# Four unread bf16 products per recurrent step, and one semaphore for both inputs of the cell scan

## The chip, the core and the metric

The kernel runs on one core of a Trainium2 chip. The time is device microseconds of that core, the median of three runs. The engines of a core are TensorE (PE for its products, PEld for its weight loads), VectorE (DVE), ScalarE (ACT), GpSimd (POOL) and SyncE (SP, which here only issues DMAs); each runs its own list of instructions and waits for others on semaphores.

## The reference

A graph of 6250 nodes with 256 features goes through four residual blocks: a weighted neighbour sum, a mixture of eight expert layers, a four-head graph attention, and an LSTM that walks over the 6250 nodes one after the other. Only the last one matters here:

```python
def step(carry, xp):                  # 6250 times, each on the h and c of the one before
    h, c = carry
    gates = xp + h @ W_hh.T           # 256 -> 1024
    i, f, g, o = jnp.split(gates, 4, axis=-1)
    c = sigmoid(f) * c + sigmoid(i) * tanh(g)
    h = sigmoid(o) * tanh(c)
    return ((h, c), h)
```

`xp` is `x @ W_ih.T` plus both biases for all nodes, computed ahead of the loop.

## The kernel before, in words

The kernel is a list of stages, one after the other: `stage_places`, `stage_scatter`, `stage_items` (sorting of edges), `stage_aggregate`, `stage_experts`, `stage_heads`, `stage_maxima`, `stage_attend`, `stage_project` (writes `xp` to HBM), `stage_lstm` (the recurrence) and `stage_finish`. The change is in `stage_lstm` alone.

`stage_lstm` gives each engine its own loop of 625 turns with 10 steps each (PER = CH * LU = 2 * 5). A step, engine by engine:

- TensorE first writes the `xp` row of the step into three PSUM banks (f, i and g, o; two sets of banks, used in turn) by three f32 products with a 128 x 128 selection matrix `sel` and 64 columns of `xp` (line 1160). Each is recorded as two weight loads and two matmuls, so six of each. Then it waits for `h_ready`, and adds h @ W_hh.T: the weights loaded into the array are h itself (one or two columns of it), the columns that stream are 64 columns of `ls_w`, and four such products lie side by side in the four 32-column parts of the array (`tile_position=(0, 32 * j)`). There are 8 of them for f (line 1167), 16 for i and g (1173) and 8 for o (1178), each recorded as two: 16, 32 and 16 matmuls. After each of the three blocks `gates_ready` goes up.
- VectorE transposes the f bank, the i/g bank and the o bank into SBUF (1229, 1233, 1235; each raises `turned`), waits for `f_mul` and for `ig_act`, runs one scan that makes the new cell state (1239), waits for `tc_ready` and writes the new h into the ring `ls_ht` (1242, raises `h_ready`).
- ScalarE takes tanh of f (1188, raises `f_act`), of i and g straight into the scan's input (1190, raises `ig_act`), of o (1192), of the new cell state (1194, raises `tc_ready`), and copies that state to the scan's input (1195). Every fifth step it copies five h to the history (1199).
- GpSimd multiplies tanh(f) by the old cell state into the scan's input (1147, raises `f_mul`).
- SyncE loads five rows of `xp` at a time into one half of a double buffer when `xp_used` says it is free.

Sigmoids are written as tanh of half the argument; the weights are scaled for that. PSUM banks 0 to 5 hold the gates; banks 6 and 7 are not used in this stage.

Of the kernel before, what the change touches and what calls it, by code (L numbers as in the profile page):

```python
# [14 lines left out]
BF16 = mybir.dt.bfloat16  # L15
I32 = mybir.dt.int32
ALU = mybir.AluOpType
ACT = mybir.ActivationFunctionType
# [3 lines left out]
P = 128  # L22
# [1082 lines left out]
def stage_lstm(nc, sb, sem, g):  # L1105
# [4 lines left out]
    tf_cols, ti_cols, to_cols = sb("ls_f_cols", [P, HD]), sb("ls_ig_cols", [P, HD]), sb("ls_o_cols", [P, HD])  # L1110
    tf, to, tc = sb("ls_tf", [P, 2]), sb("ls_to", [P, 2]), sb("ls_tc", [P, 2])
    SC = 5
    d = sb("ls_d", [P, 2, 2 * SC + 1])
    cell = sb("ls_cell", [P, 2 * SC])
    ht = sb("ls_ht", [P, 2 * LU, 2, 3])
    free = sb("ls_free", [P, 1])
    d1, d0 = d[:, 0, 1:2 * SC + 1], d[:, 1, 0:2 * SC]
    c_now = cell[:, SC - 1:2 * SC:SC]
    banks_f, banks_ig, banks_o = [[g["ps"][3 * s + k] for s in range(2)] for k in range(3)]
    w_loaded, zeroed, gates_ready, turned, f_act, f_mul, ig_act, scanned, tc_ready, h_ready, kept, xp_used = (sem("ls_" + n) for n in (  # L1120
        "w_loaded", "zeroed", "gates_ready", "turned", "f_act", "f_mul", "ig_act", "scanned", "tc_ready", "h_ready", "kept", "xp_used"))
    xp_in = [sem("ls_xp0"), sem("ls_xp1")]
    PER = CH * LU
    with nc.Block() as block:
# [15 lines left out]
        @block.gpsimd  # L1140
        def _(pool):
            pool.memset(free[:, :], 0.0).then_inc(kept, 2)
            pool.wait_ge(zeroed, 5)
            with pool.Fori(0, N // PER) as i:
                for k in range(PER):
                    pool.wait_ge(f_act, i * PER + (k + 1))
                    nc.gpsimd.tensor_tensor(d1[:, 2:2 * SC:SC], tf[:, :], c_now, ALU.mult).then_inc(f_mul, 1)  # L1147

        @block.tensor
        def _(pe):  # L1150
            pe.wait_ge(zeroed, 5)
            with pe.Fori(0, N // PER) as i:
                for k in range(PER):
                    q, u, s = k // LU, k % LU, k % 2
                    b = q % 2
                    if u == 0:
                        pe.wait_ge(xp_in[b], i * (CH // 2 * 16) + (q // 2 + 1) * 16)

                    for bank, lo in ((banks_f[s], HD), (banks_ig[s], 0), (banks_o[s], HD)):
                        x = nc.tensor.matmul(bank[:, 0:HD], sel[:, u, :], xp[:, b, lo:lo + HD], start=True, stop=False)  # L1160
                    if u == LU - 1:
                        x.then_inc(xp_used, 1)
                    pe.wait_ge(h_ready, i * PER + (k + 1))
                    v = (k - 1) % (2 * LU)
                    for c in range(2):
                        for j in range(4):
                            m = nc.tensor.matmul(banks_f[s][32 * j:32 * j + 1, 0:HD], ht[:, v, c, 1:2], w[:, c, j, HD:2 * HD],  # L1167
                                                 start=False, stop=c == 1, tile_position=(0, 32 * j))
                    m.then_inc(gates_ready, 1)
                    for r, lo in ((0, 0), (1, 2 * HD)):  # L1170
                        for c in range(2):
                            for j in range(4):
                                m = nc.tensor.matmul(banks_ig[s][32 * j:32 * j + 2, 0:HD], ht[:, v, c, 1 - r:3 - r], w[:, c, j, lo:lo + HD],  # L1173
                                                     start=False, stop=(r, c) == (1, 1), tile_position=(0, 32 * j))
                    m.then_inc(gates_ready, 1)
                    for c in range(2):
                        for j in range(4):
                            m = nc.tensor.matmul(banks_o[s][32 * j:32 * j + 2, 0:HD], ht[:, v, c, 0:2], w[:, c, j, 3 * HD:4 * HD],  # L1178
                                                 start=False, stop=c == 1, tile_position=(0, 32 * j))
                    m.then_inc(gates_ready, 1)  # L1180

        @block.scalar
        def _(act):
            act.wait_ge(zeroed, 5)
            with act.Fori(0, N // PER) as i:
                for k in range(PER):
                    act.wait_ge(turned, i * (3 * PER) + (3 * k + 1))
                    nc.scalar.activation(tf[:, :], tf_cols[:, 0:33:32], ACT.Tanh).then_inc(f_act, 1)  # L1188
                    act.wait_ge(turned, i * (3 * PER) + (3 * k + 2))
                    nc.scalar.activation(d[:, :, 2:3 + SC:SC], ti_cols[:, :].rearrange("p (c m) -> p m c", c=2)[:, 0:2, :], ACT.Tanh).then_inc(ig_act, 1)  # L1190
                    act.wait_ge(turned, i * (3 * PER) + (3 * k + 3))
                    nc.scalar.activation(to[:, :], to_cols[:, 1:34:32], ACT.Tanh)  # L1192
                    act.wait_ge(scanned, i * PER + (k + 2))
                    nc.scalar.activation(tc[:, :], c_now, ACT.Tanh).then_inc(tc_ready, 1)  # L1194
                    nc.scalar.copy(d1[:, 3:2 * SC:SC], c_now)
                    if k % LU == LU - 1:
                        v = k % (2 * LU) - (LU - 1)
                        act.wait_ge(h_ready, i * PER + (k + 2))
                        nc.scalar.copy(g["HIST"][:, :, ds(i * PER + (k - LU + 1), LU)], ht[:, v:v + LU, :, 1].rearrange("p u c -> p c u")).then_inc(kept, 1)

        @block.vector
        def _(dve):
            vec = nc.vector
            vec.memset(xp[:, :, :], 0.0).then_inc(zeroed, 1)
            vec.memset(sel[:, :, :], 0.0).then_inc(h_ready, 1)
            vec.memset(cell[:, :], 0.0)
            vec.memset(d[:, :, :], 0.0).then_inc(scanned, 1)
            dve.wait_ge(h_ready, 1)
            for j in range(4):
                for r in range(2):  # L1210
                    m = vec.tensor_copy(sel[:, :, 32 * j + r], g["ident"][:, 2 * j + r:2 * j + r + R * (LU - 1) + 1:R])
            m.then_inc(zeroed, 1)
            vec.memset(ht[:, :, :, :], 0.0)
            dve.wait_ge(scanned, 1)
            vec.memset(d1[:, 0:2 * SC:SC], 1.0)
            vec.memset(d0[:, 1:2 * SC:SC], 1.0)
            vec.memset(d0[:, 3:2 * SC:SC], 1.0)
            vec.memset(d0[:, 4:2 * SC:SC], 0.5)
            dve.wait_ge(w_loaded, 16)

            for lo, hi, scale in ((0, 2 * HD, 0.25), (2 * HD, 3 * HD, 0.5), (3 * HD, D, 0.25)):
                v = w[:, :, :, lo:hi].rearrange("p c j n -> p (c j) n")
                vec.tensor_scalar(v, v, scale, None, ALU.mult).then_inc(zeroed, 1)  # L1223
            dve.wait_ge(zeroed, 5)
            with dve.Fori(0, N // PER) as i:
                for k in range(PER):
                    s = k % 2
                    dve.wait_ge(gates_ready, i * (3 * PER) + (3 * k + 1))
                    vec.transpose(tf_cols[:, :], banks_f[s][:, 0:HD]).then_inc(turned, 1)  # L1229
                    if k % LU == 0:  # L1230
                        dve.wait_ge(kept, i * CH + (k // LU + 1))
                    dve.wait_ge(gates_ready, i * (3 * PER) + (3 * k + 2))
                    vec.transpose(ti_cols[:, :], banks_ig[s][:, 0:HD]).then_inc(turned, 1)  # L1233
                    dve.wait_ge(gates_ready, i * (3 * PER) + (3 * k + 3))
                    vec.transpose(to_cols[:, :], banks_o[s][:, 0:HD]).then_inc(turned, 1)  # L1235
                    dve.wait_ge(f_mul, i * PER + (k + 1))
                    dve.wait_ge(ig_act, i * PER + (k + 1))

                    vec.tensor_tensor_scan(cell[:, :], d0, d1, 0.0, ALU.mult, ALU.add).then_inc(scanned, 1)
                    dve.wait_ge(tc_ready, i * PER + (k + 1))  # L1240

                    vec.scalar_tensor_tensor(out=ht[:, k % (2 * LU), :, 1], in0=to[:, :], scalar=1.0, in1=tc[:, :],  # L1242
                                             op0=ALU.add, op1=ALU.mult).then_inc(h_ready, 1)
# [135 lines left out]
def build(nc, ins, out):  # L1379
    with ExitStack() as ctx:  # L1380
# [24 lines left out]
        with ExitStack() as items:  # L1405
# [21 lines left out]
            stage(stage_project)  # L1427
        g["HIST"] = keep("history", [P, 2, N])
        stage(stage_lstm)
        stage(stage_finish)  # L1430

# [12 lines left out]
```

## Time and profile before

| | |
|---|---|
| median of 3 runs | 31179.84 us (31170.26 to 31184.28) |
| profiled execution | 31181.4 us, span 31179.7 us |
| PE / PEld busy over the span | 84% / 70% |
| DVE / ACT / POOL busy | 36% / 27% / 25% |
| mean granted TensorE clock | 0.631 of full speed |
| recurrent stage, first to last instruction | about 10466 to 31014 us, 6250 steps |

The page divides the span into 40 slices of 780 us; a digit is the busy share of a slice in tenths, and PEclk is the granted clock of TensorE in tenths. The clock has two levels, 1.2 and 2.4 GHz, shown as 0.50 and 1.00; a value between is a mixture over the stretch. PE's busy time counts a matmul from its start to the end of its latency, so PE can show 100% while the array itself has pauses.

### The profile page before, as it was taken

The page shows a single profiled execution, that of the slowest core. Times are in us where ns is not written, and L with a number is a line of the kernel's source. Part 1 is how long each engine was busy: PE and PEld are TensorE (multiplying, and loading weights), DVE is VectorE, ACT ScalarE, POOL GpSimd, SP SyncE. Part 2 cuts the span into 40 slices and gives each one's busy share as a digit, 9 for nine tenths or more (in the row PEclk, how much of TensorE's full clock was granted, in tenths as well). Part 3 has the DMA queues.
Part 4 walks back from the last instruction along what each step waited for, and adds up shares of the span by engine and source line. Part 5 has one row for each costly group of instructions (what it writes and reads, how often), then busy time and mean ns, then how long its engine had stood idle before and what let it go on. Part 6 is the DMA issues. An engine that isn't in the chain of part 4 may idle for free. (4 is left out here: it accounts for less than half of the span.)

```text
span 31179.7 us, 1124934 instructions
## 1 busy us (share of the span) xinstructions
PE 26082.7 (84%) x456492; PEld 21913.3 (70%) x456597; DVE 11210.6 (36%) x40897; ACT 8537.5 (27%) x40793; POOL 7747.7 (25%) x12838
## 2 busy tenths in 40 slices
PE   0002556788777799999999999999999999999998
PEld 0002334333665688888888888888888888888887
DVE  7002333777555333333333333333333333333334
ACT  0000001688111132222222222232222222222322
POOL 1776771677776000000000000000000000000000
PEclk9998778999888655555555555555555555555555
DMA  0002331000333000000000000000000000000000
GB/s 36 1 1 71 104 105 24 7 2 2 97 99 93 33 1 1 1 1 1 1 1 1 1 1 1 1 1 1 1 1 1 1 1 1 1 1 1 1 1 9
DMA packets 370440, 557.74 MB, mean 18 GB/s; under 512 B 177610, under 2 KB 254830, under 8 KB 369006
## 3 DMA queue, kind: packets, MB, share of 16 engines
q0 software_dynamic: 263728, 458.62, 5.9%
q1 hardware_dynamic: 106686, 98.81, 1.0%
q8 instruction: 11, 0.18, 0.0%
q14 instruction: 15, 0.12, 0.0%
HBM read 496.64 MB, written 60.32 MB: 18 GB/s over the span
## 5 line engine op out<-in xcount | busy, mean ns | idle before, releaser
L1160 PE MATMUL banks<-ls_xp,ls_sel 128*128 128x64 f32 x37500 | 9641.6, 430 | 18.2 <-DVE ls_w L1223 18.2
L1160 PEld LDWEIGHTS banks<-ls_xp,ls_sel 128*128 128x128 f32 x37500 | 8466.7, 325 | 1376.1 <-issue 1376.1
L1173 PE MATMUL banks<-ls_w,ls_ht 128*2 128x64 f32 x200000 | 6735.4, 311 | 0.0
L1147 POOL TENSOR_TENSOR ls_d<-ls_tf,ls_cell 128x2 f32<-128x2 f32 x6250 | 1241.9, 199 | 19305.7 <-ACT ls_tf L1188 19305.7
L1173 PEld LDWEIGHTS banks<-ls_w,ls_ht 128*2 128x2 f32 x200000 | 5585.4, 127 | 0.0
L1229 DVE STREAM_TRANSPOSE ls_f_cols<-banks 128x64 f32<-128x64 f32 x6250 | 1561.5, 250 | 7590.1 <-PE banks L1167 7590.1
L1178 PE MATMUL banks<-ls_w,ls_ht 128*2 128x64 f32 x100000 | 4068.7, 311 | 0.0
L436 PE MATMUL banks<-ag_rows,ag_pick 128*128 128x256 f32 x3328 | 1204.8, 526 | 3392.9 <-DMA ag_rows<-y_table,ag_idx 3359.0
L1167 PE MATMUL banks<-ls_w,ls_ht 128*1 128x64 f32 x100000 | 3777.1, 299 | 0.0
L1188 ACT ACTIVATE ls_tf<-ls_f_cols 128x2 f32<-128x2 f32 x6250 | 1286.8, 206 | 8783.7 <-DVE ls_f_cols L1229 8776.7
L436 PEld LDWEIGHTS banks<-ag_rows,ag_pick 128*128 128x128 f32 x3328 | 831.5, 262 | 3765.6 <-DMA ag_rows<-y_table,ag_idx 2759.9
L1178 PEld LDWEIGHTS banks<-ls_w,ls_ht 128*2 128x2 f32 x100000 | 2918.7, 127 | 0.0
L1233 DVE STREAM_TRANSPOSE ls_ig_cols<-banks 128x64 f32<-128x64 f32 x6250 | 1561.5, 250 | 3771.8 <-PE banks L1173 3771.8
L1167 PEld LDWEIGHTS banks<-ls_w,ls_ht 128*1 128x1 f32 x100000 | 1975.0, 103 | 736.4
L1190 ACT ACTIVATE ls_d<-ls_ig_cols 128x4 f32<-128x4 f32 x6250 | 1313.6, 210 | 3849.5 <-DVE ls_ig_cols L1233 3849.5
L1235 DVE STREAM_TRANSPOSE ls_o_cols<-banks 128x64 f32<-128x64 f32 x6250 | 1561.5, 250 | 1105.2 <-PE banks L1178 1105.2
L389 POOL DMA_INDIRECT at_rows<-wh_table,at_idx x1664 | 1743.2, 1048 | 511.1 <-issue 477.3
L389 POOL DMA_INDIRECT mx_rows<-alpha_dst_table,mx_idx x1664 | 1657.0, 996 | 507.7 <-issue 459.8
L329 POOL DMA_INDIRECT rec_table<-st_rec,st_idx x1560 | 1495.1, 958 | 1034.4 <-ACT st_idx L304 559.4
L389 POOL DMA_INDIRECT ag_rows<-y_table,ag_idx x1664 | 1582.0, 951 | 515.8 <-issue 497.9
L1192 ACT ACTIVATE ls_to<-ls_o_cols 128x2 f32<-128x2 f32 x6250 | 1278.3, 205 | 1353.1 <-DVE ls_o_cols L1235 1353.1
L1242 DVE SCALAR_TENSOR_TENSOR ls_ht<-ls_to,ls_tc 128x2 f32<-128x2 f32 x6250 | 1017.3, 163 | 1695.1 <-ACT ls_tc L1194 1695.1
(256 smaller groups left out, 19365.3 us busy)
## 6 DMA issues: line engine op xcount, KB each, us to landing
ag_rows<-y_table,ag_idx POOLq DMA_INDIRECT x1664, 2.7
mx_rows<-alpha_dst_table,mx_idx POOLq DMA_INDIRECT x1664, 2.3
at_rows<-wh_table,at_idx POOLq DMA_INDIRECT x1664, 2.8
projections<-xp_out SPq DMA_DIRECT2D x7, 3584.0 KB, 10.4
rec_table<-st_rec,st_idx POOLq DMA_INDIRECT x1563, 2.1
ls_xp<-projections SPq DMA_DIRECT2D x1250, 20.0 KB
rec_table<-zero POOLq DMA_DIRECT2D x5, 2496.0 KB, 20.9
rec_part<-rec_table SPq DMA_DIRECT2D x5, 2496.0 KB, 19.9
```

What stands on the lines that cost most here:

```text
L329: pool.indirect_dma_start(g["rec"][k], bass.IndirectOffsetOnAxis(ap=idx[:, h, u % SH:u % SH + 1], axis=0), recs[:, h, u % SH, :], None).th ...
L389: pool.indirect_dma_start(rows[:, u, :], None, table, bass.IndirectOffsetOnAxis(ap=idx[:, u // HU, u % HU:u % HU + 1], axis=0)).then_inc(g ...
L436: m = nc.tensor.matmul(sums[k], pick[:, u, :], rows[:, u, :], start=u == 2 * k, stop=u == 2 * k + 1)
L1160: x = nc.tensor.matmul(bank[:, 0:HD], sel[:, u, :], xp[:, b, lo:lo + HD], start=True, stop=False)
L1167: m = nc.tensor.matmul(banks_f[s][32 * j:32 * j + 1, 0:HD], ht[:, v, c, 1:2], w[:, c, j, HD:2 * HD], start=False, stop=c == 1, tile_positi ...
L1173: m = nc.tensor.matmul(banks_ig[s][32 * j:32 * j + 2, 0:HD], ht[:, v, c, 1 - r:3 - r], w[:, c, j, lo:lo + HD], start=False, stop=(r, c) == ...
L1178: m = nc.tensor.matmul(banks_o[s][32 * j:32 * j + 2, 0:HD], ht[:, v, c, 0:2], w[:, c, j, 3 * HD:4 * HD], start=False, stop=c == 1, tile_po ...
L1188: nc.scalar.activation(tf[:, :], tf_cols[:, 0:33:32], ACT.Tanh).then_inc(f_act, 1)
L1190: nc.scalar.activation(d[:, :, 2:3 + SC:SC], ti_cols[:, :].rearrange("p (c m) -> p m c", c=2)[:, 0:2, :], ACT.Tanh).then_inc(ig_act, 1)
L1229: vec.transpose(tf_cols[:, :], banks_f[s][:, 0:HD]).then_inc(turned, 1)
L1233: vec.transpose(ti_cols[:, :], banks_ig[s][:, 0:HD]).then_inc(turned, 1)
L1235: vec.transpose(to_cols[:, :], banks_o[s][:, 0:HD]).then_inc(turned, 1)
```

## The change

- A bf16 tile `wake` of 128 x 512 is added and set to 1.0 once, ahead of the loop.
- In each step, after the three `xp` products and ahead of the wait for `h_ready`, TensorE issues four bf16 products: one column of `wake` as the weights, 512 columns of `wake` streaming, each in another 32-column part of the array, into four rows of PSUM bank 6. Nobody reads bank 6 and no semaphore is raised.
- `f_mul` (POOL) and `ig_act` (ACT) become one semaphore `scan_in`, raised once by each in each step; the scan waits once, for `2 * (k + 1)` instead of twice for `k + 1`.

```diff
+    wake = sb("ls_wake", [P, 512], BF16)
...
-                    nc.gpsimd.tensor_tensor(d1[:, 2:2 * SC:SC], tf[:, :], c_now, ALU.mult).then_inc(f_mul, 1)
+                    nc.gpsimd.tensor_tensor(d1[:, 2:2 * SC:SC], tf[:, :], c_now, ALU.mult).then_inc(scan_in, 1)
...
                     if u == LU - 1:
                         x.then_inc(xp_used, 1)
+                    for j in range(4):
+                        nc.tensor.matmul(g["ps"][6][32 * j:32 * j + 1, :], wake[:, 0:1], wake[:, :], start=True, stop=True, tile_position=(0, 32 * j))
                     pe.wait_ge(h_ready, i * PER + (k + 1))
...
-                    nc.scalar.activation(d[:, :, 2:3 + SC:SC], ti_cols[:, :].rearrange("p (c m) -> p m c", c=2)[:, 0:2, :], ACT.Tanh).then_inc(ig_act, 1)
+                    nc.scalar.activation(d[:, :, 2:3 + SC:SC], ti_cols[:, :].rearrange("p (c m) -> p m c", c=2)[:, 0:2, :], ACT.Tanh).then_inc(scan_in, 1)
...
             vec.memset(ht[:, :, :, :], 0.0)
+            vec.memset(wake[:, :], 1.0)
...
-                    dve.wait_ge(f_mul, i * PER + (k + 1))
-                    dve.wait_ge(ig_act, i * PER + (k + 1))
+                    dve.wait_ge(scan_in, i * (2 * PER) + (2 * k + 2))
```

## Rows read from the trace of the kernel before

**Rows 1.** The page's 40 slices: TensorE granted clock, in tenths.
```profile
PEclk9998778999888655555555555555555555555555
```
**Rows 2.** Stretch, its length, busy PE, PEld, DVE, ACT, POOL; then clock, DMA share, GB/s.
```profile
10105.00:10130.00 25.00, 21.70 (x51) 9.31 (x49) 9.04 (x14) 0.00 (x0) 0.00 (x0) 1.00 0.06 24
...
10466.00:31014.00 20548.00, 20541.70 (x437500) 18447.89 (x437500) 6367.92 (x31268) 6146.59 (x33121) 1241.86 (x6250) 0.50 0.00 1
```
**Rows 3.** Timeline of one step: start, duration, engine, line, operation, count, idle before.
```profile
20000.22 1.54 PE L1160 MATMUL banks<-ls_xp,ls_sel 128*128 128x64 f32 x6
...
20000.53 0.17 DVE L1239 TENSOR_TENSOR_SCAN ls_cell<-ls_d 128x10 f32<-128x10 f32 x1
...
20000.75 0.19 ACT L1194 ACTIVATE ls_tc<-ls_cell 128x2 f32<-128x2 f32 x1
...
20000.98 0.16 DVE L1242 SCALAR_TENSOR_TENSOR ls_ht<-ls_to,ls_tc 128x2 f32<-128x2 f32 x1 [0.27 <-ACT ls_tc L1194]
...
20001.69 0.60 PE L1167 MATMUL banks<-ls_w,ls_ht 128*1 128x64 f32 x16
...
20002.07 1.08 PE L1173 MATMUL banks<-ls_w,ls_ht 128*2 128x64 f32 x32
20002.36 0.25 DVE L1229 STREAM_TRANSPOSE ls_f_cols<-banks 128x64 f32<-128x64 f32 x1 [1.23 <-PE banks L1167]
20002.65 0.20 ACT L1188 ACTIVATE ls_tf<-ls_f_cols 128x2 f32<-128x2 f32 x1 [1.62 <-DVE ls_f_cols L1229]
...
20002.92 0.65 PE L1178 MATMUL banks<-ls_w,ls_ht 128*2 128x64 f32 x16
20002.93 0.20 POOL L1147 TENSOR_TENSOR ls_d<-ls_tf,ls_cell 128x2 f32<-128x2 f32 x1 [3.09 <-ACT ls_tf L1188]
20003.22 0.25 DVE L1233 STREAM_TRANSPOSE ls_ig_cols<-banks 128x64 f32<-128x64 f32 x1 [0.60 <-PE banks L1173]
20003.50 0.21 ACT L1190 ACTIVATE ls_d<-ls_ig_cols 128x4 f32<-128x4 f32 x1 [0.65 <-DVE ls_ig_cols L1233]
...
20003.51 1.54 PE L1160 MATMUL banks<-ls_xp,ls_sel 128*128 128x64 f32 x6
...
20003.81 0.18 DVE L1239 TENSOR_TENSOR_SCAN ls_cell<-ls_d 128x10 f32<-128x10 f32 x1
```
**Rows 4.** The same timeline where a loop turn of ten steps begins.
```profile
20004.26 0.16 DVE L1242 SCALAR_TENSOR_TENSOR ls_ht<-ls_to,ls_tc 128x2 f32<-128x2 f32 x1 [0.27 <-ACT ls_tc L1194]
20004.54 0.21 ACT L1199 COPY history<-ls_ht 128x10 f32 x1 [0.22 <-DVE ls_ht L1242]
20004.96 1.28 ACT L1188 ACT_TABLE_LOAD   x1 [0.21 <-issue]
...
20006.25 0.20 ACT L1188 ACTIVATE ls_tf<-ls_f_cols 128x2 f32<-128x2 f32 x1
```
**Rows 5.** Timeline, four thin products of one group alone.
```profile
20011.93 0.33 PE L1173 MATMUL banks<-ls_w,ls_ht 128*2 128x64 f32 x4
```
**Rows 6.** Timeline, fourteen 128-column products at clock 1.00, then at clock 0.50.
```profile
5045.92 1.69 PE L124 MATMUL banks<-ident,moe_v 128*128 128x128 f32 x14
...
10150.92 3.25 PE L124 MATMUL banks<-ident,xp_xn 128*128 128x128 f32 x14 [24.21 <-DVE xp_xn L102]
```
**Rows 7.** Timeline at clock 1.00, two bf16 products of 512 columns, then one.
```profile
6101.59 0.59 PE L797 MATMUL banks<-mx_ident,mx_pen 128*128 128x512 bf16 x2
...
6104.51 0.38 PE L797 MATMUL banks<-mx_ident,mx_pen 128*128 128x512 bf16 x1 [0.60 <-ACT mx_pen L785]
```
**Rows 8.** By line and form, the fourteen of Rows 6: count, busy us, mean ns of one.
```profile
L124 PE MATMUL banks<-ident,moe_v 128*128 128x128 f32 x14 | 1.7, 272 | 0.0
...
L124 PE MATMUL banks<-ident,xp_xn 128*128 128x128 f32 x14 | 3.2, 425 | 24.2 <-DVE xp_xn L102 24.2
```
**Rows 9.** By line and form, 16000 to 20000 us: one thin product, and ScalarE's table loads.
```profile
L1173 PE MATMUL banks<-ls_w,ls_ht 128*2 128x64 f32 x38944 | 1311.5, 311 | 0.0
...
L1188 ACT ACT_TABLE_LOAD x121 | 155.2, 1283 | 25.6 <-issue 25.6
```

More of the change, by code:

```diff
@@ L1119, in stage_lstm @@
     banks_f, banks_ig, banks_o = [[g["ps"][3 * s + k] for s in range(2)] for k in range(3)]
-    w_loaded, zeroed, gates_ready, turned, f_act, f_mul, ig_act, scanned, tc_ready, h_ready, kept, xp_used = (sem("ls_" + n) for n in (
-        "w_loaded", "zeroed", "gates_ready", "turned", "f_act", "f_mul", "ig_act", "scanned", "tc_ready", "h_ready", "kept", "xp_used"))
+    w_loaded, zeroed, gates_ready, turned, f_act, scan_in, scanned, tc_ready, h_ready, kept, xp_used = (sem("ls_" + n) for n in (
+        "w_loaded", "zeroed", "gates_ready", "turned", "f_act", "scan_in", "scanned", "tc_ready", "h_ready", "kept", "xp_used"))
     xp_in = [sem("ls_xp0"), sem("ls_xp1")]
```

## The prediction

> **What bounds the kernel now.** I read the page's slices first [rows 1]. PEclk changes between 7 and 9 up to the thirteenth slice, falls to 5 at the fifteenth and stays there. The stretches say it exactly [rows 2]: the recurrent stage takes 20548 us, two thirds of the span, PE has a record open in practically all of it, and the granted clock is 0.50, the level of 1.2 GHz. 20548 us over 6250 steps is 3.287 us a step (the steps counted here by POOL's 6250 products). Elsewhere the same engine gets 1.00 (2.4 GHz) with less recorded work: 87% PE busy in 10105 to 10130 us; and the slices at 7 and 8 are mixtures of both levels.
>
> Then the timeline of one step [rows 3]. The xp products of a step start at 0.22 (us behind 20000), the recurrent products at 1.69, the next xp products at 3.51: 1.47 us for one block and 1.82 for the other, with nothing between. The new h starts at 0.98 and ends at 1.14, yet the products that need it start at 1.69. So h waits for TensorE 0.5 us in every step: the loop is bound by TensorE's own work at the low level, not by the chain through the other engines.
>
> Inside the two blocks: the six xp products start (1.54 - 0.42) / 5 = 0.22 apart (0.42 for one, from a like product in [rows 8]), though 64 columns need less; their 128-column weight loads pace them. Fourteen products with the same loads take 3.25 us at the low level and 1.69 at the high one [rows 6]; with one duration of 0.42 and 0.27 [rows 8] taken off, they are 0.217 and 0.109 apart, so this pace follows the clock. The 32 i/g products fill 2.07 to 2.92: 8 groups of four, 0.106 a group; a group alone [rows 5] lasts 0.33 against 0.311 for one product [rows 9], so the four start within 0.02 and run side by side. The 16 groups are 1.70 us of the 1.82.
>
> **The four products of ones.** They stand behind the xp products and ahead of the wait for h, so at the low level, where h is already there, they are on TensorE's path in full. Two bf16 products of 512 columns at the high level take 0.59 us together, one alone 0.38 [rows 7]: 0.21 apart. Each of the new ones streams as many columns; twice that, 0.43, at the low level, no row of before has it. Do the four overlap? They use the four column parts as [rows 5] do, so I take one duration and 0.02: 0.23 high, 0.43 to 0.45 low. In series it would be 0.85 and 1.71; these are the ends. Their weight load is one column, like line 1167's, and costs nothing that shows there. Bank 6 is nobody's, and the added VectorE fill of `wake` happens once, ahead of 6250 steps: nothing.
>
> So all depends on whether the extra columns lift the clock. In a step of before the array has columns to process for 16 x 0.106 + 6 x 0.106 = 2.33 of 3.29 us; half of the xp block is pauses between weight loads, which PE's busy row hides behind latencies. The stretch at 1.00 is one of wide products one after the other (51 in 25 us, half a microsecond each, 87% busy) [rows 2]. The change puts an unbroken run of 0.43 us right ahead of the recurrent groups, in 2.76 of 3.71 us. I take the clock to rise and to stay up, since at the high level the step is shorter and the same columns come more often.
>
> The Trainium skill ("TensorE: Matmul & The Clock Gate", section "What's actually happening") says "the default state is throttled, and activity releases the throttle". Taken for recorded busy time, that speaks against this change: [rows 2] has PE recorded busy for 20548 us at 0.50, so what counts is not what PE's row shows, and one-column weights might count for little as well. By it the sum would be the rival "clock stays low" below. Whoever counts streaming columns gets the forecast.
>
> **The step at the high level, along the chain.** Time 0 is the first f product. Low: 12 groups to the first o product take 2.92 - 1.69 = 1.23, that is 12 x 0.106 less 0.04. High: the i/g block's last group starts at 11 x 0.053 - 0.03 = 0.55. A thin product lasts 0.31 at the low level; a 128-column one went from 0.42 to 0.27 [rows 8], about half of the streaming and little of the latency, so 0.24: the i/g block ends at 0.80. The transpose of i/g follows 0.07 later (2.07 + 7 x 0.106 + 0.31 = 3.12; it starts at 3.22, so 0.07 to 0.10): 0.87. From there all is VectorE and ScalarE and does not follow TensorE's clock [rows 3]: transpose to scan 3.81 - 3.22 = 0.59, scan to tanh(c) 0.22, to the new h 0.23, its 0.16, and 0.07 from its end to the first product (as PE to DVE; before it was hidden, 0.03 to 0.10). Sum 0.87 + 0.59 + 0.22 + 0.23 + 0.16 + 0.07 = 2.14 us. The f side is earlier: f ends at 0.40, transpose 0.47, POOL's product 0.57 later (2.93 - 2.36) at 1.04, done 1.24, against 1.41 for ig_act. The o side too: its last product ends at 1.02, and by the f side's delay (2.65 - 2.36) plus 0.07 its tanh starts at 1.38, while tanh(c) is due at 1.68.
>
> **One semaphore in place of two.** tanh of i/g ends at 3.71 and the scan starts at 3.81, 0.10 later; after tanh(c), a single wait, h starts 0.98 - 0.94 = 0.04 later. The merge removes one standing wait of VectorE: between 0 and 0.07. I take 0.04. At the low level it is worth nothing (h has 0.5 us of slack); at the high level it counts: 2.10. Behind the waiting scan stands only h's own product, behind that the next transpose, so nothing new is held; POOL and ACT raise it once each per step and neither can be a step ahead, since both wait for transposes behind the scan.
>
> **Once in ten steps** ScalarE loads its tables [rows 4, 9]: 121 in 4000 us, 1.28 us each. The load starts 0.70 behind h's start and tanh(f) 1.99 behind it. At the low level h's 0.5 us of slack and the longer products hide it. At the high level tanh(f) would be due at 0.23 + 0.47 + 0.29 = 0.99 behind h's start; the product on POOL then ends at 1.99 + 0.28 + 0.20 = 2.47 and the scan starts at 2.5 rather than at 0.23 + 1.42 = 1.65: 0.85 us late, 0.085 a step. The history copy ends at 0.49, before 0.99: free. So 2.10 + 0.085 = 2.19.
>
> **What is late next is close.** TensorE's own work at the high level: groups 0.85 and 0.12 around them, xp 6 x 0.109 and 0.15 (0.19 at the low level, 1.47 - 6 x 0.213), wake 0.23: 2.00 us. It stays just under the chain's 2.10; the quartet fits in the time in which PE would wait for h. I take 2.20 for both. Saved: 3.287 - 2.20 = 1.087 us, 6250 times: 6794 us. 31181.4 - 6794 = 24387; the profiled execution is 1.6 us over the median of three, so the two are the same here. **Forecast: 24390 us.** Its own range is 2.05 (chain with the full 0.07, TensorE 2.00) to 2.42 a step, 23450 to 25800.
>
> **Rivals.**
> - *The clock stays low.* The quartet is then pure load on the engine that bounds: 3.287 + 0.43 = 3.71 us a step, +2690 us, 33870. It decides as soon as the level is 0.50, from the first step. For it: 20548 us at 0.50 under full recorded load, and weights of one column. Against: four parts of the array used side by side with all 128 rows, and 512 columns without a pause. In series it would be +10690, 41870; [rows 5] speak against that. Chance 0.17.
> - *The thin products don't get faster with the clock,* because issuing them binds: a group stays at 0.106. TensorE's step is 2.00 + 16 x 0.053 = 2.85, above the chain (2.10 + 11 x 0.053 = 2.68): 31181 - 6250 x 0.437 = 28450. For it: each group issues eight instructions. Against: the four of a group start within 0.02. Chance 0.14. The Trainium skill ("TensorE: Matmul & The Clock Gate", "Back-to-back issue gap") gives small matmuls a floor of about 25 ns from start to start, 64 x 0.025 = 1.6 us for a step's thin products, an estimate near this rival's 1.7; [rows 5] contradict it within a group, no row of before tests it over many at the high level.
> - *The quartet runs in series at the high level:* TensorE 2.00 + 0.64 = 2.64: 27140. Chance 0.05.
> - *The clock changes to and fro* as in the slices at 7 and 8 [rows 1]: half at each, (24390 + 33870) / 2 = 29130. Chance 0.06.
> - *Nothing changes* (a low clock, with the quartet in time that is free): 0.01.
>
> **How the numbers follow.** Forecast 0.57. Faster by over 0.2%, about what a measurement here can tell: 0.57 + 0.14 + 0.05 + 0.06 = 0.82; slower 0.17; same 0.01. The range from 23300 to 29500 holds all of the faster cases but the edges; left out is the slower one.
>
> **What would show it.** PEclk 1.00 through the recurrent stage; thin groups 0.053 apart; the four products of ones within 0.25 us; a gap on PE between them and the f products, ended by h; the scan 0.06 behind tanh of i/g; one step in ten longer by 0.85 us. PEclk at 0.50 with xp to f 1.90 apart would prove me wrong as a whole; groups at 0.106 with PEclk 1.00 in the size.

## The result and the profile after

The changed kernel takes 24358.47 us (median of 4, 24356.56 to 24366.54) against 31180.4 for the kernel before: a ratio of 0.7813, 95% interval 0.7799 to 0.7827. Forecast were 24390. Ahead of and behind the recurrence nothing moved: the first h is written at 10474 us as against 10476 us before, and the difference of 6825 us between the spans (31179.7 and 24354.7) lies in the recurrent stage.

First the stretch of that stage, with the columns of [rows 2], and the page's clock by slices:

```profile
10466.00:24190.00 13724.00, 13239.33 (x462500) 10810.16 (x462500) 6649.67 (x31251) 6599.39 (x33121) 1233.77 (x6250) 1.00 0.01 2
```
```profile
PEclk9999877789999888799999999999999999999999
```

13724 us over 6250 steps is 2.196 us a step, at a granted clock of 1.00 where it was 0.50 [rows 2]. Now the timeline of TensorE at the start of the stage, where the clock changes:

```profile
10469.43 1.54 PE L1161 MATMUL banks<-ls_xp,ls_sel 128*128 128x64 f32 x6 [18.19 <-DVE ls_w L1227]
10470.90 0.60 PE L1165 MATMUL banks<-ls_wake 128*1 128x512 bf16 x4
10471.28 0.65 PE L1170 MATMUL banks<-ls_w,ls_ht 128*1 128x64 f32 x16
10471.71 1.07 PE L1176 MATMUL banks<-ls_w,ls_ht 128*2 128x64 f32 x32
10472.56 0.65 PE L1181 MATMUL banks<-ls_w,ls_ht 128*2 128x64 f32 x16
10473.14 1.11 PE L1161 MATMUL banks<-ls_xp,ls_sel 128*128 128x64 f32 x6
10474.18 0.39 PE L1165 MATMUL banks<-ls_wake 128*1 128x512 bf16 x4
10474.39 0.40 PE L1170 MATMUL banks<-ls_w,ls_ht 128*1 128x64 f32 x16
...
10475.39 0.88 PE L1161 MATMUL banks<-ls_xp,ls_sel 128*128 128x64 f32 x6
10476.20 0.39 PE L1165 MATMUL banks<-ls_wake 128*1 128x512 bf16 x4
```

The first step is as slow as every step of before: six xp products in 1.54 us, sixteen thin ones in 0.65 (0.60 in [rows 3]). The second step's xp products take 1.11, the third's 0.88: the clock rises after one step with a quartet in it and has no further change until the stage is over. The quartet is recorded as 0.60 us at the low level and 0.39 at the high one.

The timeline of one plain step in the middle, on all engines, answers to [rows 3]:

```profile
20003.22 0.39 PE L1165 MATMUL banks<-ls_wake 128*1 128x512 bf16 x4
20003.30 0.16 DVE L1245 SCALAR_TENSOR_TENSOR ls_ht<-ls_to,ls_tc 128x2 f32<-128x2 f32 x1 [0.27 <-ACT ls_tc L1197]
...
20003.52 0.40 PE L1170 MATMUL banks<-ls_w,ls_ht 128*1 128x64 f32 x16
...
20003.74 0.63 PE L1176 MATMUL banks<-ls_w,ls_ht 128*2 128x64 f32 x32
...
20004.18 0.41 PE L1181 MATMUL banks<-ls_w,ls_ht 128*2 128x64 f32 x16
...
20004.44 0.25 DVE L1237 STREAM_TRANSPOSE ls_ig_cols<-banks 128x64 f32<-128x64 f32 x1 [0.20 <-PE banks L1176]
...
20004.52 0.88 PE L1161 MATMUL banks<-ls_xp,ls_sel 128*128 128x64 f32 x6
...
20004.96 0.18 DVE L1242 TENSOR_TENSOR_SCAN ls_cell<-ls_d 128x10 f32<-128x10 f32 x1
20005.17 0.21 ACT L1197 ACTIVATE ls_tc<-ls_cell 128x2 f32<-128x2 f32 x1
...
20005.41 0.16 DVE L1245 SCALAR_TENSOR_TENSOR ls_ht<-ls_to,ls_tc 128x2 f32<-128x2 f32 x1 [0.27 <-ACT ls_tc L1197]
20005.63 0.22 PEld L1170 LDWEIGHTS banks<-ls_w,ls_ht 128*1 128x1 f32 x16 [0.21 <-DVE ls_ht L1245]
```

From h to h it is 20005.41 - 20003.30 = 2.11 us. Note who waits now: the weight load at 20005.63 has an idle time before it that h ended, while before h was ready half a microsecond ahead of TensorE. The bound has moved from TensorE's work to the chain through all engines.

And the step with the table load, by three starts of h on VectorE:

```profile
19996.13 0.16 DVE L1245 SCALAR_TENSOR_TENSOR ls_ht<-ls_to,ls_tc 128x2 f32<-128x2 f32 x1 [0.27 <-ACT ls_tc L1197]
19998.24 0.16 DVE L1245 SCALAR_TENSOR_TENSOR ls_ht<-ls_to,ls_tc 128x2 f32<-128x2 f32 x1 [0.27 <-ACT ls_tc L1197]
20001.19 0.16 DVE L1245 SCALAR_TENSOR_TENSOR ls_ht<-ls_to,ls_tc 128x2 f32<-128x2 f32 x1 [0.27 <-ACT ls_tc L1197]
```

2.11, then 2.95: 0.84 us more, once in ten steps.

### The profile page after: what moved, and what is told of

The parts are those of the page before. It is cut to its first block and busy times, and to the rows that moved or that the text cites. A ratio compares the mean times of both kernels' runs of the same rounds, so it can differ in the third digit from the quotient of the medians.

```text
span 24354.7 us, 1174935 instructions
## 1 busy us (share of the span) xinstructions
PE 18767.2 (77%) x481492; PEld 14260.6 (59%) x481597; DVE 11493.8 (47%) x40898; ACT 8989.8 (37%) x40793; POOL 7736.8 (32%) x12838
## 5 line engine op out<-in xcount | busy, mean ns | idle before, releaser
L1161 PE MATMUL banks<-ls_xp,ls_sel 128*128 128x64 f32 x37500 | 5508.6, 283 | 84.3 <-DVE ls_w L1227 18.2
L1161 PEld LDWEIGHTS banks<-ls_xp,ls_sel 128*128 128x128 f32 x37500 | 4654.0, 191 | 854.6 <-issue 198.6
L1176 PE MATMUL banks<-ls_w,ls_ht 128*2 128x64 f32 x200000 | 3930.9, 219 | 0.0
L1176 PEld LDWEIGHTS banks<-ls_w,ls_ht 128*2 128x2 f32 x200000 | 3093.2, 85 | 0.0
L1170 PE MATMUL banks<-ls_w,ls_ht 128*1 128x64 f32 x100000 | 2520.5, 218 | 414.2 <-DVE ls_ht L1245 414.1
L1181 PE MATMUL banks<-ls_w,ls_ht 128*2 128x64 f32 x100000 | 2534.7, 219 | 0.6 <-issue 0.6
L1165 PE MATMUL banks<-ls_wake 128*1 128x512 bf16 x25000 | 2419.3, 377 | 0.0
L1170 PEld LDWEIGHTS banks<-ls_w,ls_ht 128*1 128x1 f32 x100000 | 1404.0, 82 | 1653.6 <-DVE ls_ht L1245 1630.7
L1181 PEld LDWEIGHTS banks<-ls_w,ls_ht 128*2 128x2 f32 x100000 | 1697.2, 85 | 0.8 <-issue 0.8
L802 PE MATMUL banks<-mx_diag,mx_pick 128*128 128x512 f32 x3328 | 1566.5, 593 | 0.0
```

The source lines that it names most:

```text
L802: m = nc.tensor.matmul(ps[u % 8][:, :], pick[:, u, :], diag[:, u, :, :].rearrange("p h e -> p (h e)"), start=False, stop=True)
L1165: nc.tensor.matmul(g["ps"][6][32 * j:32 * j + 1, :], wake[:, 0:1], wake[:, :], start=True, stop=True, tile_position=(0, 32 * j))
```

## The experiments

Twelve kernels ran, in three groups of four, the first and third on chip 0, the second on chip 14. The kernel before, run beside them, takes 32054, 31175 and 32142 us. The difference lies ahead of the recurrence; one of the stages that gather rows by indirect DMA shows it (3000 to 4000 us: 104 GB/s in the trace of before, 91 in the first group). The recurrence at the low level took 20548 us in the trace of before and 20539 us in that of the first kernel below, where the kernel as a whole is 3% slower, so I compare the length of the recurrence and its steps.

**The merged semaphore alone.**

```diff
-                    for j in range(4):
-                        nc.tensor.matmul(g["ps"][6][32 * j:32 * j + 1, :], wake[:, 0:1], wake[:, :], start=True, stop=True, tile_position=(0, 32 * j))
```

> The merged semaphore without the four products. My theory (all of the gain is TensorE's clock, and at the low level TensorE bounds the step): the clock stays at 0.50, a step stays at 3.287 us, 31180 us within 0.2%. Rival (the wait of the scan was worth part of it): a shorter step at 0.50, up to 0.07 us of 3.287, so down to 30740.

32063.75 us beside 32054 for the kernel before, all four executions within 18 us. The recurrent stage:

```profile
11362.00:31901.00 20539.00, 20537.85 (x437429) 18444.37 (x437428) 6120.22 (x31246) 6069.19 (x33122) 1232.96 (x6249) 0.50 0.00 1
```

Clock 0.50 and 3.287 us a step: at the low level the merge is worth nothing, so the gain comes from the products of ones.

**The four products, with the two semaphores of before.**

```diff
+                    dve.wait_ge(f_mul, i * PER + (k + 1))
+                    dve.wait_ge(ig_act, i * PER + (k + 1))
-                    dve.wait_ge(scan_in, i * (2 * PER) + (2 * k + 2))
```

> The four products with the two semaphores of before. Theory: the clock is 1.00 through the recurrence, and the merge is worth 0.04 us of the chain in nine steps of ten, so 24358 + 6250 x 0.04 = 24600. Bounds: 24360 (the merge is worth nothing) and 24800 (0.07 in every step). Rival (TensorE's own 2.03 us bounds the step, not the chain): no difference to the changed kernel.

25632.46 us on that chip, a recurrence of 14102 us at clock 1.00. Against 13724 that is 378 us, 0.06 a step: a plain step takes 2.18 us instead of 2.11, the one with the table load 2.95 as before. Two rows of VectorE show where:

```profile
20003.84 0.25 DVE L1237 STREAM_TRANSPOSE ls_ig_cols<-banks 128x64 f32<-128x64 f32 x1 [0.20 <-PE banks L1176]
...
20004.44 0.18 DVE L1243 TENSOR_TENSOR_SCAN ls_cell<-ls_d 128x10 f32<-128x10 f32 x1
```

Transpose to scan is 0.60 (0.59 in [rows 3]); merged it is 20004.96 - 20004.44 = 0.52. So the merge is worth 0.07 in a plain step (0.04 was forecast, 0.07 its upper bound) and nothing in the long one, where the scan waits for POOL's product. The rival, that TensorE bounds the step, is out: the merge would then show nothing.

**One product instead of four.**

```diff
-                    for j in range(4):
+                    for j in range(1):
```

> One of the four products of ones, in one column part of the array, with the merged semaphore; it streams as long as the four did side by side. Theory A (what lifts the clock is that columns stream, however wide the array is used): clock 1.00, 24360. Theory B (the part of the array in use decides, so a quarter is too little): clock 0.50 and 0.43 us more a step, 31180 + 2670 = 33850.

25245.52 us where the kernel before takes 32054. The recurrence:

```profile
11350.00:25074.00 13724.00, 13228.92 (x443678) 10707.84 (x443677) 6649.69 (x31245) 6595.75 (x33120) 1233.20 (x6249) 1.00 0.01 2
```

13724 us at clock 1.00, to the microsecond that of the changed kernel. One column part of the array is enough; the width in use did not decide. Three of the four products are ballast. They cost nothing, since they run beside the first.

**The products only ahead of the loop.**

```diff
+            for j in range(128):
+                nc.tensor.matmul(g["ps"][6][32 * (j % 4):32 * (j % 4) + 1, :], wake[:, 0:1], wake[:, :], start=True, stop=True, tile_position=(0, 32 * (j % 4)))
             with pe.Fori(0, N // PER) as i:
...
-                    for j in range(4):
-                        nc.tensor.matmul(g["ps"][6][32 * j:32 * j + 1, :], wake[:, 0:1], wake[:, :], start=True, stop=True, tile_position=(0, 32 * j))
```

> The products of ones stand 128 times ahead of the loop (32 groups, 14 us at the low level) and not at all in a step; merged semaphore. Theory A (at the high level a step takes 2.11 us and not 3.29, so its own products come often enough to hold the level; only the start needs help): clock 1.00 to the end, 24360 + 10. Theory B (each step needs the products, the thin ones count for little): the clock falls to 0.50 soon after the loop begins, 31190.

25253.9 us, four executions within 23 us. The burst, the first steps and the whole stage:

```profile
11343.40 9.19 PE L1154 MATMUL banks<-ls_wake 128*1 128x512 bf16 x128 [18.07 <-DVE ls_w L1227]
11352.51 0.88 PE L1163 MATMUL banks<-ls_xp,ls_sel 128*128 128x64 f32 x6
```
```profile
11355.00:25079.00 13724.00, 11825.36 (x437426) 10198.70 (x437425) 6649.67 (x31246) 6595.88 (x33120) 1233.26 (x6249) 1.00 0.01 2
```

The same 13724 us, with not one product of ones in 6250 steps. In this loop, which has no gap of microseconds, the level holds itself: the kernel's own work, one step in 2.11 us, keeps it; only to rise from the low level did it need help.

That has a consequence for the kernel before, and its runs beside the experiments show it. Of 27, 25 are at mean clocks of 0.62 to 0.63; one of the first group took 25736.94 us at 0.929, and one 30256.16 us at 0.698. No trace of these two is kept, but 25737 us is close to the 25632 of the same two semaphores with the quartet. By that the kernel before can run its recurrence at the high level; it seldom gets there.

**Columns in the quartet: 256 and 128 instead of 512.**

```diff
-                        nc.tensor.matmul(g["ps"][6][32 * j:32 * j + 1, :], wake[:, 0:1], wake[:, :], start=True, stop=True, tile_position=(0, 32 * j))
+                        nc.tensor.matmul(g["ps"][6][32 * j:32 * j + 1, 0:256], wake[:, 0:1], wake[:, 0:256], start=True, stop=True, tile_position=(0, 32 * j))
```

> The four products stream 256 columns instead of 512. If the clock is lifted all the same, the time is that of the changed kernel (the chain bounds, a shorter quartet frees nothing): 25250 on a chip with the slower other stages. If it is too little, the clock stays at 0.50 and a step takes 3.287 + 0.22 = 3.51 us: 1400 us over the kernel before, 33450. In between, executions that differ from one another.

24360.11 us, four executions within 6 us. The clock rises 14 us, or four steps, later than in the changed kernel, and then stays:

```profile
10474.00:10488.00 14.00, 14.00 (x297) 12.43 (x298) 4.03 (x21) 3.33 (x21) 0.79 (x4) 0.50 0.02 4
10488.00:24196.00 13708.00, 13035.38 (x462130) 10754.98 (x462130) 6643.09 (x31226) 6594.50 (x33099) 1232.73 (x6245) 1.00 0.01 2
```

> The four products stream 128 columns instead of 512. With 256 the clock rose about six steps later than with 512. If the columns in a step decide when the clock rises: it rises later still, or in some executions only; once it has risen it stays, 2.11 us a step. Then either 24360 to 24500, or values up to 31500 that differ from run to run. If any extra work is enough: 24360 as with 256 columns.

With 128 columns three executions took 32763 to 32784 us at clock 0.62 and one 25357 at 0.926. The profiled one stayed low from end to end:

```profile
11454.00:32617.00 21163.00, 21162.75 (x462425) 19060.94 (x462424) 6134.32 (x31244) 6101.09 (x33118) 1243.31 (x6249) 0.50 0.00 1
```

21163 / 6250 = 3.386 us a step, 0.10 over the 3.287 of before. Here my slow rival happened: the price of a quartet that does not lift the clock. A quarter of the 0.43 us that I put on the full quartet is 0.107. The full quartet itself stood at the low level in one step only, the changed kernel's first: 10471.28 - 10470.90 = 0.38 us, so 0.43 was somewhat high.

**Two quartets.**

```diff
-                    for j in range(4):
-                        nc.tensor.matmul(g["ps"][6][32 * j:32 * j + 1, :], wake[:, 0:1], wake[:, :], start=True, stop=True, tile_position=(0, 32 * j))
+                    for j in range(8):
+                        nc.tensor.matmul(g["ps"][6][32 * (j % 4):32 * (j % 4) + 1, :], wake[:, 0:1], wake[:, :], start=True, stop=True, tile_position=(0, 32 * (j % 4)))
```

> Eight products of ones a step instead of four, else the changed kernel. It measures how near TensorE's own work is to the bound. When h did not make it wait (third step of the changed kernel) TensorE's step was 0.21 + 1.00 + 0.81 = 2.02 us against the chain's 2.11. Theory: a second quartet adds 0.21, so a plain step takes 2.24 us, the step with the table load stays at 2.95, and the recurrence takes 6250 x 0.9 x 0.13 = 730 us more than with one quartet. Rival (the wait for h hides the quartets whatever their number): no difference.

26260.76 us, beside 31175 for the kernel before on that chip. A plain step takes 2.24 us, as expected, and the long one 2.95. But the recurrence takes 15595 us, where 13724 + 730 = 14450 were forecast. At 125 of the 625 turns of the loop TensorE stands still for some 5 us. Without these gaps ten steps take 22.97 us; each gap costs (15595 - 625 x 22.97) / 125 = 9.9 us with the slow steps behind it. TensorE's timeline and the DMA queues (12000 to 24000 us) show why:

```profile
10630.40 0.40 PE L1181 MATMUL banks<-ls_w,ls_ht 128*2 128x64 f32 x16
10635.75 1.54 PE L1161 MATMUL banks<-ls_xp,ls_sel 128*128 128x64 f32 x6 [4.96 <-issue]
10637.22 1.02 PE L1165 MATMUL banks<-ls_wake 128*1 128x512 bf16 x8
10638.92 0.60 PE L1170 MATMUL banks<-ls_w,ls_ht 128*1 128x64 f32 x16 [0.68 <-issue]
```
```profile
q8 instruction: 880, 14.42, 0.6%
```

Nothing that the profile shows makes TensorE wait for these 5 us; the queue by which instructions are loaded, which has no entry in this stretch of the changed kernel, moves 14 MB. Behind the gap the clock is low (1.54 for six xp products) and rises again.

**As many instructions, but short ones.**

```diff
+                    for j in range(4):
+                        nc.tensor.matmul(g["ps"][6][32 * j:32 * j + 1, 0:16], wake[:, 0:1], wake[:, 0:16], start=True, stop=True, tile_position=(0, 32 * j))
```

> The quartet of the changed kernel and four more products of only 16 columns. The two-quartet kernel had 14 MB of instruction DMA on TensorE's queue in 12 ms and gaps of 5 us, the changed kernel none. Theory (the stalls come from the number of instructions in TensorE's ten-step body, not from the time they take): as many instructions as with two quartets, so the same fetches and gaps in about 250 of 625 turns, with plain steps of 2.11 to 2.15 us: 24358 + 250 x 7 = 26100, less up to some hundred. Rival (the stalls come with the longer quartet): no fetches, 24400.

25836 us twice and 28428 and 28451 us, on a chip where the kernel before takes 32142. Plain steps of 2.11 us, and fetches again:

```profile
q8 instruction: 355, 5.82, 0.2%
```

So the number of instructions in the body brings the gaps, not the time they take. The profiled execution, one of the shorter two, has 49 gaps of some 5 us; they cost (14216 - 13724) / 49 = 10.0 us each. The 250 turns of the forecast were too many, since with two quartets it was 125. Why the executions differ, and why this one has fewer gaps than with two quartets, is open.

**Fifty steps in the body of every engine's loop.**

```diff
-CH = 2
+CH = 10
```

> The loop body holds 50 steps instead of 10 (CH = 10), else the changed kernel. Theory: the tables are loaded once per turn of the loop, 125 times instead of 625, and each load costs the step 2.95 - 2.11 = 0.84 us: 420 us less than the changed kernel on the same chip (25250 becomes 24830 where its other stages are as slow as in the last group of runs). Rival (the long step comes from the turn of the loop or from the history copy, or fetching a body five times as long costs time): the same time or more.

25746.65 us where the kernel before takes 31175: not 420 us less than the changed kernel but 1388 more. My theory of the load was right in its size and wrong in what a longer body costs. Queues from 12000 to 24000 us, and the gap at a turn of the loop:

```profile
q8 instruction: 3062, 50.17, 1.8%
...
q14 instruction: 1186, 9.72, 0.3%
```
```profile
20011.60 1.54 PE L1161 MATMUL banks<-ls_xp,ls_sel 128*128 128x64 f32 x6 [4.63 <-issue]
```

The step at a turn takes 9.4 us, the next two 3.7 and 2.6, and steps in between lose up to a microsecond.

**Fifty steps, and the products only ahead of the loop.**

```diff
-CH = 2
+CH = 10
...
-                    for j in range(4):
-                        nc.tensor.matmul(g["ps"][6][32 * j:32 * j + 1, :], wake[:, 0:1], wake[:, :], start=True, stop=True, tile_position=(0, 32 * j))
+            for j in range(128):
+                nc.tensor.matmul(g["ps"][6][32 * (j % 4):32 * (j % 4) + 1, :], wake[:, 0:1], wake[:, :], start=True, stop=True, tile_position=(0, 32 * (j % 4)))
```

> No product of ones in a step, 128 of them ahead of the loop, and the body of 50 steps. If both effects are as thought, they don't disturb each other: clock 1.00 throughout, a plain step 2.11 us, 125 table loads: as the 50-step body with quartets, 24830 on a chip with the slower other stages. If the clock falls somewhere, each step behind it takes 3.287 us.

30881.69 us. This is the run that tells what the quartet in each step is for:

```profile
10582.61 0.41 PE L1181 MATMUL banks<-ls_w,ls_ht 128*2 128x64 f32 x16
10587.52 1.54 PE L1163 MATMUL banks<-ls_xp,ls_sel 128*128 128x64 f32 x6 [4.51 <-issue]
...
10595.15 1.54 PE L1163 MATMUL banks<-ls_xp,ls_sel 128*128 128x64 f32 x6
```
```profile
10480.00:30714.00 20234.00, 19494.31 (x437424) 17425.20 (x437424) 6154.43 (x31246) 5516.31 (x32619) 1236.32 (x6249) 0.54 0.02 5
```

The clock falls behind the first gap at a turn, and without quartets it comes back only now and then: mean clock 0.54. The trace has 15 later stretches at the high level, each 106 us long: one turn of fifty steps, from just behind one gap to the next. Why the clock rises behind some gaps and not behind others is open. With quartets and the same gaps it was 0.94 (the fifty-step kernel above), back after each within some steps.

**A longer body for ScalarE alone: 30 and 40 steps.**

```diff
-            with act.Fori(0, N // PER) as i:
-                for k in range(PER):
+            AP = 30
...
+            with act.Fori(0, N // AP) as i:
+                steps(i * AP, AP)
+            steps(N // AP * AP, N % AP)
```

> ScalarE's loop alone gets a body of 30 steps (208 turns and ten steps behind them); TensorE's body keeps its ten. Theory (a table load at each turn of ScalarE's loop costs 0.84 us, and what made the 50-step body slow was fetching TensorE's instructions): 209 loads instead of 625, 416 x 0.84 = 350 us less: 24358 becomes 24010 on a chip where the changed kernel takes 24358, no instruction DMA in the recurrence. Rival (a longer body of any engine has to be fetched anew at each turn): stalls of some us at each of 208 turns, slower than the changed kernel.

25012.07 us where the kernel before takes 32141.63, a ratio of 0.7782 (0.7771 to 0.7793). The recurrence takes 13411 us at clock 1.00, 313 less than the changed kernel's 13724, and the instruction queues have no entry from 12000 to 24000 us:

```profile
11434.00:24845.00 13411.00, 13204.71 (x462425) 10805.51 (x462425) 6649.94 (x31245) 6158.17 (x32704) 1233.72 (x6249) 1.00 0.01 2
```

Forecast were 350 less. Table loads now come once in 30 steps; but two of those 30, where the other engines' loops of ten turn and the history is copied, take 2.20 instead of 2.11, which the load had covered: 417 x 0.09 = 37 us.

> The same with 40 steps in ScalarE's body (156 turns and ten steps). If 40 steps still need no fetching: 157 loads, 468 x 0.84 = 390 us less, 23970. If they do: instruction DMA in the recurrence and one stall of 3 us or more at each turn, which eats what is saved, about 24400.

25692.56 us, a recurrence of 14078: slower than the changed kernel's. One step in forty takes 5.1 us:

```profile
20018.93 0.21 ACT L1204 COPY history<-ls_ht 128x10 f32 x1 [0.22 <-DVE ls_ht L1251]
20021.55 1.28 ACT L1193 ACT_TABLE_LOAD   x1 [2.41 <-issue]
```
```profile
20024.02 0.40 PE L1170 MATMUL banks<-ls_w,ls_ht 128*1 128x64 f32 x16 [2.91 <-DVE ls_ht L1251]
```
```profile
q14 instruction: 666, 5.46, 0.2%
```

The load stands 2.41 us behind the copy instead of 0.21 [rows 4]: ScalarE's own body has to be fetched. Between 30 and 40 steps lies its end. The fetch costs the clock too: TensorE idles for 2.8 to 3.2 us at each of 155 turns, and each time the granted clock falls to 0.50 for some steps (0.97 over the stage). With 30 steps no idle time between TensorE's products reaches 0.8 us in the recurrence, and the clock stays at 1.00.

The Trainium skill ("Runtime: NRT & Kernel Launch", "Instruction fetch mechanics") gives the instruction memory as 32 KiB for most engines and 128 KiB for TensorE, filled in blocks, and says that a taken branch whose target is not in the blocks at hand "forces a DMA fetch of the target page". The forty-step run moved 5.46 MB in 5325 steps, 1.03 KB a step: an estimate of 31 KB for 30 steps and 41 KB for 40, on either side of the page's figure. TensorE's fifty-step run moved 50.17 MB in 4938 steps, 10.2 KB a step: by the same estimate 102 KB for ten steps, which need no fetch, and with the eight more instructions a step some 107 KB, which do. These are upper ends, since more than the body may be fetched: in 12000 to 24000 us the two-quartet run moved 14.42 MB at 98 gaps, 147 KB each. Even so a body well under 128 KiB had to be fetched. There the measurement decides, and no run here shows where exactly the end is.

## Why the prediction was right

Step by step, in its order.

- *What bounds.* TensorE's own work at the low level: shown by the merged semaphore alone, which shortens the chain and gains nothing there, and by the 0.10 us a step that the quartets of 128 columns cost.
- *The clock rises and stays.* Right. The reason given, that streaming columns count and not what PE's row shows, has support but is not shown: one 512-column product did as much as four, and fewer columns did it later or seldom. No run separates the number of columns from the length of the unbroken run of them, or bf16 from f32. That 512 would suffice was a bet, as the 0.57 says: no row of before told how much is enough, and with 128 columns it would have been lost in three executions of four. The objection that I took from the Trainium skill, recorded busy time, fell: with the products only in front, PE is recorded busy 86% of the stage (11825 of 13724) and keeps 1.00, while at 100% [rows 2] it got 0.50. What I missed: I spoke of columns that come more often at the high level, but did not draw the conclusion that the kernel before could hold it too, as it seems to have done in one of 27 executions.
- *The quartet overlaps.* 0.39 us for four, 0.377 for one: right.
- *Thin products follow the clock.* The i/g block takes 4.18 - 3.74 = 0.44 for 8 groups, 0.055 each, 0.053 said. With 64 products in 0.88 us, 14 ns each, the floor of 25 ns that the Trainium skill gives ("TensorE: Matmul & The Clock Gate", "Back-to-back issue gap") does not hold for four products side by side.
- *The chain.* Said 2.10, measured 2.11, and partly by two errors that cancel: from the first f product to the i/g transpose it is 4.44 - 3.52 = 0.92, not 0.87; the merge is worth 0.07, the upper bound, not 0.04. Scan to h 0.45 and h to the first product 0.22 were 0.45 and 0.23. In the comparison with the f side, tanh of i/g was due at 0.87 + 0.49 = 1.36, not 1.41; nothing hangs on it.
- *The table load.* 0.84 a time for 0.85.
- *What is late next.* In the second to third step, where h came early, TensorE's round was 0.21 + 1.00 + 0.81 = 2.02 (said 2.00), and a second quartet made it the bound at 2.24. The 0.09 us between it and the chain is all there is.

Sum: 2.196 a step, 2.20 said, 24358 us for 24390.

## What to carry to other kernels

Where a long loop of small products runs at the low level of TensorE's clock although PE is never without a record, a few wide unread products in time that is free at the high level can lift it there. If they don't lift it, they cost: the quartets of 128 columns made the kernel 2% slower in three executions of four. Try also whether they are needed throughout or only ahead of the loop, and keep them in the loop when gaps of some microseconds can occur. Count the instructions of a loop body before making it longer: eight more a step brought gaps of 5 us. Each engine's loop may have its own length, and ScalarE's should be as long as needs no fetching, since here it loads its tables once a turn (1.28 us, 0.84 on the chain).

The version to keep is the changed kernel with 30 steps in ScalarE's body: its recurrence is 313 us shorter. The two were not run beside each other.

## What was not expected of the hardware

- Both levels of the clock are stable for the same loop: 3.287 us a step at 0.50, 2.11 to 2.18 at 1.00. The kernel before, by time and mean clock, ran at the high level once; one more execution (30256 us, 0.698) lies in between and seems to have changed within the stage.
- A TensorE body of ten steps fits, eight instructions a step more do not, and the cost is a gap of 5 us on TensorE that the profile puts down to "issue", together with entries of the instruction queue. The gap also costs the high level for some steps, and so does a wait of TensorE for 2.9 us that a fetch of ScalarE's brings.
- The three groups of runs differ by up to 3% of the whole time (31175, 32054 and 32142 us for the kernel before), all of it ahead of the recurrence; a gathering stage there ran at 104 or 91 GB/s.
